# A decoder layer on one core: setup, projections and the loop's first passes merged into one block that works by pairs of chunks

## What is computed

```python
h = rms(x, w_norm_in)                                   # the kernel also makes z = layernorm(x)
conv = conv_b + sum(hp[:, j:j + T, :] * conv_w[:, j] for j in range(4))   # causal, 4 taps
h = silu(conv)
q = (h @ wq).reshape(B, T, 8, 64);  k = (h @ wk).reshape(B, T, 8, 64);  v = (h @ wv)...
q = q / (norm(q) + 1e-6);  k = k / (norm(k) + 1e-6)     # over the 64 of a head
sd = h @ w_spike
ab = silu(h @ w_au + b_au) @ w_ad + b_ad;  bb = h @ w_beta + b_beta
# for every token t in turn:
mem = 0.9 * mem + sd[t];  hard = mem > 0.5;  mem = mem - 0.5 * hard      # the scan
alpha = sigmoid(ab[t] + alpha_spike * hard);  beta = sigmoid(bb[t] + sum(hard * beta_spike))
alpha, beta = (alpha, beta) if any(hard) else (1, 0)
s = s * alpha;  s = s - beta * k (k.s) + beta * k v;  out = s.q
```

## Time and profile before

| | before |
|---|---|
| median of 3 runs | 1237.21 us (1233.9 to 1239.5) |
| the profiled execution | 1248.79 us, span 1247.1 us |
| mean granted TensorE clock | 0.93 |
| busy: TensorE, VectorE, ScalarE, GpSimd | 87%, 59%, 40%, 16% |

### The profile page before, as it was taken

The page is one execution under the profiler, slowest core; times in us unless marked ns, Lnnn a source line. Parts: engine busy times, 40 slices in busy tenths (PEclk is TensorE's granted clock), DMA queues, the critical chain, the costliest instruction groups (busy, mean ns, idle before and its releaser), DMA issues. The chain is left out here.

```text
span 1247.1 us, 40866 instructions
## 1 busy us (share of the span) xinstructions
PE 1078.8 (87%) x17220; PEld 773.9 (62%) x17220; DVE 733.6 (59%) x2539; ACT 499.3 (40%) x1429; POOL 202.3 (16%) x381
## 2 busy tenths in 40 slices
PE   1587546999999999999999999699999899899987
PEld 1222124888888888888888887346556545644652
DVE  4656688668888888888877763127135333512710
ACT  1465201134444444444454444244235325525421
POOL 4100021112211222122221221202101101200210
PEclk9989655589999999999999998899899899999999
DMA  2000000000000000000000000300000000000000
GB/s 84 0 1 0 1 0 1 2 4 3 4 4 4 3 4 4 4 3 4 4 4 26 5 4 3 117 8 1 1 9 1 10 1 9 9 1 1 1 9 8
DMA packets 11219, 11.35 MB, mean 9 GB/s; under 512 B 1515, under 2 KB 9311, under 8 KB 11039
## 3 DMA queue, kind: packets, MB, share of 16 engines
q1 hardware_dynamic: 11039, 8.75, 2.3%
HBM read 7.70 MB, written 1.05 MB: 7 GB/s over the span
## 5 line engine op out<-in xcount | busy, mean ns | idle before, releaser
L1027 ACT COPY work<-banks 128x128 f32<-128x128 f32 x160 | 43.0, 269 | 168.3 <-PE banks L881 168.3
L851 PE MATMUL banks<-work 64*64 64x64 f32 x3072 | 103.6, 234 | 5.3 <-DVE gates L725 4.4
L881 PE MATMUL banks<-work,gates 64*64 64x32 f32 x2560 | 105.8, 221 | 2.5 <-issue 2.5
L901 PE MATMUL banks<-work 64*64 64x32 f32 x2560 | 105.9, 223 | 0.4 <-ACT work L1027 0.4
L302 DVE SCALAR_TENSOR_TENSOR mom<-gates 128x16 f32<-128x16 f32 x512 | 101.4, 198 | 5.7
L298 DVE SCALAR_TENSOR_TENSOR gates<-mom,gates 128x16 f32<-128x16 f32 x512 | 96.6, 189 | 11.4 <-ACT gates L414 6.7
L881 PEld LDWEIGHTS banks<-work,gates 64*64 64x64 f32 x2560 | 93.7, 139 | 15.3 <-issue 12.8
L725 DVE COPY_PREDICATED gates<-work,banks 128x256 f32<-128x256 uint32 x192 | 101.8, 530 | 1.1
L730 DVE TENSOR_TENSOR work<-work,banks 128x128 f32<-128x128 f32 x128 | 36.8, 288 | 104.5 <-PE banks L891 103.1
L891 PEld LDWEIGHTS banks<-work 64*64 64x64 f32 x2048 | 74.7, 140 | 33.1 <-issue 22.6
L901 PEld LDWEIGHTS banks<-work 64*64 64x64 f32 x2560 | 92.6, 140 | 0.5 <-ACT work L1027 0.5
(11 more groups left out here) (228 smaller groups left out, 2360.6 us busy)
## 6 DMA issues: line engine op xcount, KB each, us to landing
work<-in_x_dram SPq DMA_DIRECT2D x4, 256.0 KB, 2.9
out_dram<-work SPq DMA_DIRECT2D x4, 256.0 KB, 2.3
gates<-in_w_ff_dram SPq DMA_DIRECT2D x3, 256.0 KB, 3.6
wv_sb<-in_wv_dram SPq DMA_DIRECT2D x1, 512.0 KB, 4.5
work<-in_w_out_dram SPq DMA_DIRECT2D x1, 512.0 KB, 4.2
gates<-in_x_Wq_dram SPq DMA_DIRECT2D x1, 512.0 KB, 5.2
gates<-in_x_Wk_dram SPq DMA_DIRECT2D x1, 512.0 KB, 5.1
gates<-in_x_Wv_dram SPq DMA_DIRECT2D x1, 512.0 KB, 6.0
```

What stands on the lines that cost most here:

```text
L851: last = pe.matmul(level_out(l)[to, a], KS[rows, n.two, hp], late[rows, hp], start=True, stop=True)
L881: last = pe.matmul(packed(psZX, l)[rows, hp], EA[rows, n.three, l, hp], first_half(X, l)[rows, hp], start=True, stop=True)
L901: last = pe.matmul(packed(psXT, l)[rows, hp], Z[rows, l - 1, hp], second_half(XT[:, n.two], l)[rows, hp], start=True, stop=True)
L1027: ac.copy(first_half(Z[:, l - 1], l), packed(psZX, l)).then_inc(z_ok, 1)
```

## The change

The three first blocks become one. What it does:

- x is loaded in four DMAs, one for each *pair* of chunks (128 tokens of every batch, `PAIR`, `NPAIR = 4`), ahead of the weights.
- Norms: VectorE only sums the rows; ScalarE squares them with the mean as bias and a sum on the side (`square_rows`); GpSimd makes all factors in one chain (`scales`, for pair 0 before the last mask, for pairs 1 to 3 behind the masks); ScalarE applies them (`normal`, `centred`).
- Convolution: four accumulating matmuls for each pair with diagonal matrices of the taps (`taps`, `convolve`), with the sigmoid straight from PSUM. VectorE has one product per pair (`keep_h`). TensorE issues nothing before the first transposes: no matmul whose result is unread stands in the time in which the first rows' norms are computed.
- Projections go by pair in place of batch. The norms' root and reciprocal are made twice: for pair 0, and for pairs 1 to 3 together. The scalings of pair 0 lie beside the gates, those of pairs 1 to 3 in the loop's first two passes (`ramp`).
- The scan's 128 first steps and gates 0 to 3 are written out ahead of the loop, mixed with that work; the loop begins with i = -3.
- Buffers move (zeroing of `EA`, `Z` and `state` is later and waits for their earlier users); all twelve further drives come at the end of the projections.

In the core of the diff below stand, in this order: the loop's passes, GpSimd's factors, VectorE's list, TensorE's (the convolution, the part of `body` where VectorE has `four_scales` in the same place, and the list), ScalarE's list.

```diff
-            for i in range(-7, ROUNDS + 1):
+            for i in range(-3, ROUNDS + 1):
                 body(*[at_round(i + k) for k in (-1, 0, 1, 2, 3)], at_gate(i + 7), at_gate(i + 6),
-                     at_scan(i + 11))
+                     at_scan(i + 11), i + 3 if i < -1 else None)
...
+                def scales(first, n, done):
...
+                    gp.tensor_tensor(inv_std[:, cols], spread_eps[:, cols], half[:, cols], ALU.pow).then_inc(st, 1)
...
+                    gp.tensor_tensor(r2[:, cols], spread_eps[:, cols], half[:, cols], ALU.pow).then_inc(st, 1)
...
+                for l in range(LEVELS - 1):
+                    keep_late(l)
+                scales(0, 1, 0)
+                keep_late(LEVELS - 1)
...
+                scales(1, NPAIR - 1, 7)
...
+                keep_h(0)
+                done = scan_to(10, 0)
+                keep_au(0)
+                done = scan_to(14, done)
+                keep_h(1)
...
+                spikes(first[0])
+                invert(0)
+                drive(first[0])
+                spikes(first[1])
+                done = scan_to(2, done)
+                alpha(first[0])
+                for j in range(3):
+                    scale(0, j)
...
+                done = scan_to(2 * C - done, done)
+                invert(1)
                 rounds(body)
...
+                def convolve(k):
+                    pe.wait_ge(h0_ok, k + 1)
...
+                    for j in range(PAD + 1):
+                        last = pe.matmul(bank[k % 2][:, :], conv_diag[:, j, :], h0T[:, :, k * PAIR + j:k * PAIR + j + PAIR],
+                                         start=j == 0, stop=j == PAD)
...
+                        if ramp == 0 and l != 3:
+                            spread_norm(1 + l // 4, (l % 4) // 2 if l < 4 else l - 4)
+                        if ramp == 1 and l < 3:
+                            spread_norm(3, l - 1)
...
+                turn_in(0)
+                pe.wait_ge(w_loaded, 16 * 10)
+                convolve(0)
+                for n in range(HP):
+                    drive_in(n)
+                gate_in(0)
+                project(0, 2)
+                turn_in(1)
+                convolve(1)
...
+                for k in range(NPAIR):
+                    turn_z(k)
+                project(8, 4)
+                spike_sums(first[0])
+                spread_norm(0, 0)
+                project(12, 1)
+                beta_sums(first[0])
...
+                project(30, 2)
+                drive_in(HP)
+                drive_in(HP + 1)
+                sum_squares(3, 1)
+                for n in range(HP + 2, NSD):
+                    drive_in(n)
                 rounds(body)
...
+                square_rows(0)
+                square_rows(1)
+                square_rows(2)
+                taps()
+                normal(0)
+                square_rows(3)
+                keep_h0(0)
+                stairs()
+                soft_conv(0)
+                for n in range(HP):
+                    keep_drive(n)
+                normal(1)
+                soft_au(0)
+                keep_qk(0, 2)
...
+                soft_au(3)
+                norm_root(0)
+                centred(0)
+                centred(1)
+                keep_z(0)
...
+                keep_qk(8, 4)
+                soft_alpha(first[0])
...
+                keep_qk(23, 9)
+                norm_root(1)
+                for n in range(HP, NSD):
+                    keep_drive(n)
                 rounds(body)
```

More of the change, by code:

```diff
@@ new lines, in scan_to, with invert @@
+                def scan_to(steps, done):
+                    for t in range(done, done + steps):
+                        charge(ve, t)
+                        fire(ve, t)
+                    return done + steps
+                def invert(n):
+                    ve.wait_ge(nrm_ok, n + 1)
+                    if n:
+                        ve.wait_ge(bc_mm, 2)
+                    ve.tensor_scalar(nrm_e, nrm, 1e-6, None, ALU.add).then_inc(nrm_add, 1)
+                    ve.wait_ge(nrm_add, n + 1)
+                    ve.reciprocal(nrm_e, nrm_e).then_inc(nrm_inv, 1)
@@ new lines, in _ @@
+                keep_h(3)
+                done = scan_to(8, done)
+                keep_au(3)
+                done = scan_to(C - done, done)
+                spikes(first[0])
[6 more added lines that the diff above has]
+                    scale(0, j)
+                done = scan_to(1, done)
+                beta(first[0])
+                scale(0, 3)
@@ new lines, in _ @@
+                done = scan_to(2, done)
+                drive(first[1])
+                spikes(first[2])
+                done = scan_to(2, done)
+                alpha(first[1])
+                for j in range(4, 7):
+                    scale(0, j)
+                done = scan_to(1, done)
+                beta(first[1])
+                scale(0, 7)
+                done = scan_to(2, done)
+                drive(first[2])
+                spikes(first[3])
+                done = scan_to(2, done)
@@ L828, in _ @@
+                alpha(first[2])
+                done = scan_to(5, done)
+                beta(first[2])
+                done = scan_to(4, done)
+                drive(first[3])
+                done = scan_to(2, done)
+                alpha(first[3])
+                done = scan_to(2 * C - done, done)
+                invert(1)
                 rounds(body)
@@ new lines, in sum_squares @@
+                def sum_squares(k, h):
+                    pe.wait_ge(sq_ok, k * NQK + GROUPS * h + GROUPS)
+                    if k == 0 and h == 0:
+                        pe.wait_ge(sd_ok, HP)
+                        pe.wait_ge(pick_ok, 3)
+                    if k == 1 and h == 0:
+                        pe.wait_ge(nrm_ok, 1)
+                    at = ROWS - norm_row(k, h)
+                    for g, rows in enumerate(group_rows):
+                        last = pe.matmul(bank[SS_BANK][rows, :], pick[:, at:at + ROWS], sq_buf[:, GROUPS * h + g, :],
+                                         start=k <= 1 and h == 0, stop=k in (0, NPAIR - 1) and h == 1, skip_group_check=True)
+                    last.then_inc(ss_mm, 1)
@@ new lines, in stairs, with normal @@
+                def stairs():
+                    ac.wait_ge(folded, NFOLD)
+                    for g, rows in enumerate(group_rows):
+                        last = ac.copy(spread[rows].rearrange("p (r d) -> p r d", d=DK),
+                                       ident[rows, ROWS * g:ROWS * g + NROW].unsqueeze(2).broadcast_to([ROWS, NROW, DK]))
+                    last.then_inc(spread_ok, 1)
+                def normal(k):
+                    ac.wait_ge(std_ok, 2 if k == 0 else 4)
+                    for b in range(B):
+                        col = slice(k * B + b, k * B + b + 1)
+                        last = ac.activation(hn(k)[:, b], of_pair(xn, k)[:, b], ACT.Identity, bias=bh[:, col], scale=rr[:, col])
+                    last.then_inc(hn_ok, 1)
@@ L1096, in keep_out, with body @@
                             .then_inc(yout_ok, 1)
-                def body(prev, cur, nxt, aft, aft2, gate, gate_old, scan):
+                def body(prev, cur, nxt, aft, aft2, gate, gate_old, scan, ramp):
                     for l in range(1, NINV + 1):
```

737 lines of the change are left out of this document (411 added, 326 removed).

## The result

The changed kernel takes 1190.9 us (median of 4 runs, 1183.7 to 1195.7) against 1238.4 us of the kernel before (4 runs, 1233.9 to 1255.5): a ratio of 0.962, 95% interval 0.955 to 0.969, 47.4 us less. The forecast was 1191. A repetition later gave 1191.0 (6 runs) and 0.963 [0.958, 0.967].

The account below looks back on a forecast made before the run. The front was taken as a chain from engine to engine, later rounds as TensorE's. 67.8 us gained ahead of the mark less 21.5 given back make 46.3: 1202.5 profiled, 1191 as median after 11.6 off; range 1166 to 1214.

Parts of the forecast that it names:

- mark: End of the second reciprocal, where VectorE enters the pass with i = -3; forecast at 122.7 us against 190.5 before.
- wait of the first scaling: At the loop's entry VectorE idles 4.7 us until TensorE's last drives are done.
- given back in the ramp: Loop's first two passes: 15.4 us of moved scalings plus waits of 4.7 and 1.4 us, together 21.5 us.
- The front: Everything ahead of the loop is a chain between engines; first scan step at 28.5 us against 57.17.
- The stall behind the first reciprocal: VectorE waits about 4 us for the first gate's alpha, plus 3 us for slow TensorE after its gap.
- One sign against itself: Prediction is wrong if VectorE idles much over 10 us between the first and the 128th scan step.
- The other signs: Wrong if second root follows the 128th step or first passes run at full clock; first diagonal group near 145 us expected.
- by 2 us only: Before the loop, projections end near 112 and the root at 114 us, covered by the scan by 2 us.
- Rival (b): TensorE comes warm into the rounds: 18 us if all gained, giving 1173, half likelier; chance 0.16.
- Rivals (c) to (e): (c) half-clock TensorE holds prologue, 1206, 0.25; (d) half clock from first convolution, 1261, 0.03; (e) no merge overlap, 1230, 0.04.
- The offset: Old median 1237.2 lay 11.6 us below its profiled execution; the same was taken off 1202.5, giving 1191.
- The rules: Rows over skill pages: a table switch costs 1.3 us, not 2.66; GpSimd memsets do not hold the scan steps.

Follow-up runs that it names:

- e1: Changed kernel with 46 unread 128-column matmuls on TensorE ahead of the first transposes; 1188.3 us, 0.960 of the kernel before.
- e12: Changed kernel with unread matmuls at both places, ahead of the first transposes and in the loop's first two passes; 1179.2 us, 0.9522 of the kernel before.
- e8: Kernel before with only the convolution changed to TensorE matmuls, batch by batch, in its closed setup block; 1241.7 us against 1241.4, 1.003.
- e5: Changed kernel with scan steps 96 to 127 left out, so its output differs; 1200.0 us, 0.967 of the kernel before.
- e2: Changed kernel with eight drives (n = 8 to 15) moved into the loop's first pass, behind its spreads; 1198.5 us, 0.967 of the kernel before.
- e4: Changed kernel with the 24 scalings of pairs 1 to 3 and their spreads in one row ahead of the loop; 1205.6 us, 0.973 of the kernel before.

## Why the prediction was right

The time of 1191 is that of the sum, and the sum's mechanism was the one that the traces show. Two of its sizes hide each other, and the last microsecond of agreement is luck; both are told below. Term by term, as forecast, in the first execution, and in some rows in the repetition too:

| term | forecast | measured |
|---|---|---|
| first piece of x | 4.2 | 3.66 |
| factors of pair 0 | 12.8 | 12.9 |
| first transposes end | 15.6 | 16.3 |
| first convolution begins | 16.5 | 17.3, 17.0 |
| it takes | 6.0 | 6.47, 5.18 |
| first scan step | 28.5 | 29.85, 28.2 |
| first reciprocal ends | 67 | 68.6 |
| VectorE's stall behind it | 4, and 3 for the clock | 8.8, 8.1 |
| second root | 114 | 114.3 |
| mark | 122.7 | 122.4, 120.3 |
| last drive | 123 to 126 | 124.9 |
| wait of the first scaling | 4.7 | 3.7, 3.8 |
| given back in the ramp | 21.5 | 19.3, 19.2 |

**The front.** It is a chain as described, and what moves it moves the mark: in the eleven executions with all 128 steps the first step lies between 26.2 and 29.9 us, and the mark 92.0 to 93.0 us behind it. The convolution was priced by cold drives, and that was the right neighbour: it takes 5.07 to 6.71 us in the ten executions without a warm start, and 3.67 in both with one (e1, e12). The claim that the granted clock reads near full there while matmuls run at half speed held too (row 17.29:24.60 of the changed kernel: 1.00). The convolution's change of engine alone gives nothing (e8), so the gain lies in the cut into pairs, or in the two together; the prediction took both for granted without pricing them apart, and no run has the merged block with VectorE's convolution in it.

**The stall behind the first reciprocal** was mis-sized by 1.8 us. The 16 centrings and four copies that were put at 6.9 us took 9.0 (62.36 to 71.4): a centring takes 0.41 us and a copy 0.57 to 0.59, one after the other on ScalarE, and only 0.74 us are a wait for the transposes. The second half begins at 77.36 instead of 75. The forecast has it end at 122.7, 47.7 us later, but the terms that it lists (28.8, 6.4, 5.1, 2 and 3.8) add up to 46.1; measured are 45.0 (77.36 to 122.35). So the mark is met because a late start and a sum that was 1.6 too long, with terms 1.1 too high, hide each other: the parts are right to 2 or 3 us, the agreement to 0.4 is luck.

One sign against itself that the prediction named is half met. It wanted VectorE's idle time between the first and the 128th step not much over 10 us (its sum has 9: 4, 3 and 2 of small stalls); the waits come to 14.9, 11.4 of them for the sums of the gates' spikes on TensorE. The other signs are as it said: the second root (114.26) comes ahead of the last step (118.44), round 0's group at 142.9 where 145 was named, and the next two passes run at 0.66 and 0.58 of the clock.

**The entry.** That TensorE's drives and not the scan are last there was right, and e5 shows it by its size: 14.4 us of steps are taken away, and the first scaling begins at 124.06 as in the repetition. Taking the drives away is worth little alone, as the rival in e2 said, for the next spread is then late. The forecast's remark that the projections are covered "by 2 us only" was right in kind: the cover is 3.8 us (the root ends at 114.86, the last step at 118.63), and without the 32 steps they bind.

**The ramp** gave back 19.3 us instead of 21.5. From the mark to round 1 VectorE is busy 34.5 of 42.5 us, where it was busy 20.5 of 23.2. So 14.0 us more work came (15.4 forecast) and 5.3 more idle time (6.1 forecast: 4.7 and 1.4). The forecast's "nothing covers them" thus held for the scalings beside the passes' own work; e4 shows what placing them there is worth, 10.5 us against the same in a row.

**Rival (b)**, a warm TensorE in the rounds, is wrong for this change, though the first profile looked like half of it: 5.6 us gained in the pass from round 2 to 3, 4.1 in the next. The repetition has the first of them at 24.6 us, as before; the second takes 17.2 to 17.3 without the change too (e8). Where TensorE is made warm the price comes out at 6.7 and 3.2 us, 10 in all, not the 18 of the rival. It had read 7.2 and 4.1 us off a single trace, and the 4.1 are that execution's; the 3.2 are fewer because the pass comes down to 19.2 on average and not to 17.2; and its "some 7" for the first pass isn't what its own figures give (21.8 less 17.2 is 4.6), though with 15.65 us as the full-clock time it is 6.1. Rivals (c) to (e) are out by the mark.

**The offset.** The profiled execution was forecast at 1202.5 and took 1188.9: 9.7 of the 13.6 us are the clock's difference between two executions, 2.2 the ramp, 0.4 the mark, 1.3 the other rounds and the tail. The step from there to the median took over the 11.6 us by which the old profiled execution lay above its median. That step is the weak one: a single execution says nothing of how far the next kernel's profiled one will lie from its median (here 2 below). The median came out right because the median of before, too, is free of it: 1237.2 less the 46.3 of the sum. That it agrees to under 1 us is luck again: the interval of the ratio reaches from 38 to 55 us of gain, and the lead at round 1 is 48.9 us in the first execution and 51.1 in the repetition.

**The rules.** The rows first: the second table load lasts 1.28 us, and ScalarE then waits 0.23 us for TensorE and begins the root at 114.26. The Trainium skill, "ScalarE: Activation LUTs", section "What ACT_TABLE_LOAD costs", puts 2.66 us on a switch, with a drain; here the drain isn't seen, before the load or behind it. On the port: a memset of 1.81 us on GpSimd (from 114.28) left the scan steps beside it at 0.19 us, each 0.22 to 0.23 after the last. "GPSIMD Engine Reference" of the Trainium skill, section "Specifications", has contention for instructions with two SBUF inputs; beside a memset these show none, as the row of before had it. Beside GpSimd's copies they do: in the repetition the steps between 28.22 and 29.24 take 0.31 to 0.33 us (L453 copies from 28.11 to 29.19), and before 0.30 to 0.36 from 161.32 on, beside the copies of 161.23. The prediction looked at a memset only; on the path it costs some 0.4 us.

## What to carry to other kernels

Cutting a setup into pieces pays where the engines stand in a chain, and then by the length of the chain for the first piece only; a move to another engine inside a closed block may pay nothing. Work moved off a chain comes back somewhere: price the passes that take it up by what their busiest engine has free, and find which queue is last at the seam (here TensorE's drives), since only that one's length counts. A single profiled execution of a kernel whose clock wanders says where the time is, not how much it is: read the passes of two executions before a difference of the clock is put down to the change, and if a light stretch costs the clock, unread matmuls in it are cheap to try.

## What the runs showed of the hardware

- The records of the granted clock say 1.00 for the first convolution, which takes 6.47 us cold (5.07 to 6.71 in ten executions) and 3.67 after 46 unread matmuls; a first stretch of TensorE is to be read by its durations.
- Once TensorE is at half speed, two passes of small matmuls in which it is busy 93 and 98% (21.63 of 23.28, 24.15 of 24.61 us) still run at 0.50 and 0.63 of the clock. With twelve or thirteen matmuls of 512 columns in the light passes before, the first of these two runs at 0.90 to 1.00.
- The scan's operations of 128x16 take 0.27 to 0.38 us while GpSimd copies (28.11 to 29.19 in the repetition), and 0.19 beside its memsets.
- Identical instructions from round 4 to the end took 956.7 to 977.2 us in these profiles, with no clear order by kernel. That is the spread behind the medians, larger than most single edits here, and why edits of 3 us are shown by rows alone.
